# Expert results stored from ScalarE's queue two tiles later, with only weights on SyncE's queue

## What is computed

```python
logits = (xt @ Wr + br) / TEMP
probs = jax.nn.softmax(logits, axis=-1)
w, idx = jax.lax.top_k(probs, TOP_K)
w = w / jnp.clip(jnp.sum(w, axis=-1, keepdims=True), 1e-09)
comb = comb.at[jnp.arange(T)[:, None], idx].add(w)
h = jax.nn.gelu(jnp.einsum('td,edh->teh', xt, W1) + b1, approximate=False)
o = jnp.einsum('teh,eho->teo', h, W2) + b2
y = jnp.einsum('teo,te->to', o, comb)
```

## Time and profile before

| | us |
|---|---|
| median of three runs | 3003.46 (3001.4 to 3005.81) |
| the profiled execution | 2998.74 |
| its span | 2997.0 |
| PE busy | 2473.3 (83%) |
| DVE busy | 1882.4 (63%) |
| ACT busy | 1573.2 (52%) |
| POOL busy | 967.1 (32%) |
| DMA queue of SyncE | 196416 packets, 262.92 MB, 26.1% of 16 engines |

### The profile page before, as it was taken

The page is one execution under the profiler, slowest core; times in us unless marked ns, Lnnn a source line. Parts: engine busy times, 40 slices in busy tenths (PEclk is TensorE's granted clock), DMA queues, the critical chain, the costliest instruction groups (busy, mean ns, idle before and its releaser), DMA issues. The chain is left out here.

```text
span 2997.0 us, 56777 instructions
## 1 busy us (share of the span) xinstructions
PE 2473.3 (83%) x21666; PEld 1595.0 (53%) x21666; DVE 1882.4 (63%) x4197; ACT 1573.2 (52%) x2910; POOL 967.1 (32%) x725
## 2 busy tenths in 40 slices
PE   4489999999999999996877888873799999967724
PEld 2235555555555656554344666651566666744312
DVE  4578777777777766661023766754687887631285
ACT  3336666666666655554132677751377777771121
POOL 2313333333333332223000223335466666550000
PEclk8699999999999999998987899996999999978857
DMA  3301021112111100002102687744433332213020
GB/s 115 95 31 43 29 78 47 36 33 78 47 36 33 62 28 5 5 3 78 71 28 87 232 302 290 286 183 146 159 111 122 111 121 85 86 37 113 20 97 14
DMA packets 197327, 268.64 MB, mean 90 GB/s; under 512 B 48945, under 2 KB 124849, under 8 KB 196545
## 3 DMA queue, kind: packets, MB, share of 16 engines
q1 hardware_dynamic: 196416, 262.92, 26.1%
q0 software_dynamic: 640, 2.10, 0.2%
HBM read 221.18 MB, written 43.78 MB: 88 GB/s over the span
## 5 line engine op out<-in xcount | busy, mean ns | idle before, releaser
L544 POOL TENSOR_TENSOR a_plo<-a_p,a_phi 128x512 bf16<-128x512 f32 x272 | 315.6, 1160 | 815.8 <-ACT a_phi L600 814.5
L734 PE MATMUL ps<-w_hi,a_xhi 128*128 128x512 bf16 x1088 | 415.9, 382 | 0.4 <-DVE a_v L623 0.4
L735 PE MATMUL ps<-w_lo,a_xhi 128*128 128x512 bf16 x1088 | 415.5, 382 | 0.0
L736 PE MATMUL ps<-w_hi,a_xlo 128*128 128x512 bf16 x1088 | 415.2, 382 | 0.0
L1845 POOL TENSOR_TENSOR a_plo<-a_p,a_phi 128x512 bf16<-128x512 f32 x256 | 300.4, 1174 | 199.1 <-ACT a_phi L1882 198.1
L566 ACT ACTIVATE a_kraw<-ps 128x256 f32<-128x256 f32 x272 | 104.2, 383 | 412.6 <-PE ps L736 410.8
L623 DVE TENSOR_TENSOR a_v<-ps,a_v 128x256 bf16<-128x256 f32 x272 | 114.7, 422 | 261.9 <-ACT a_v L568 260.4
L1953 DVE CUSTOM_DVE_ANT_0 a_junk<-ps,a_biasrow 128x512 bf16<-128x512 f32 x256 | 175.8, 687 | 80.4 <-PE ps L2057 77.4
L1877 ACT ACTIVATE a_p<-ps,a_mcol 128x512 f32<-128x512 f32 x256 | 175.0, 684 | 86.4 <-PE ps L2075 80.1
L596 ACT ACTIVATE a_p<-ps,a_mcol 128x512 f32<-128x512 f32 x256 | 175.4, 685 | 57.0 <-PE ps L787 56.9
L1270 POOL TENSOR_TENSOR e_wlo<-e_wst,e_whi 128x2048 bf16<-128x2048 f32 x23 | 112.6, 4895 | 257.3 <-ACT e_whi L1293 257.3
(11 more groups left out here) (436 smaller groups left out, 7214.6 us busy)
## 6 DMA issues: line engine op xcount, KB each, us to landing
e_wst<-in_L_ffn_W SPq DMA_DIRECT2D x46, 2048.0 KB, 11.5
a_xn<-in_ctx SPq DMA_DIRECT2D x16, 1024.0 KB, 5.7
a_ct<-in_ctxT SPq DMA_DIRECT2D x16, 1024.0 KB, 5.5
a_ks<-k1h_d SPq DMA_DIRECT2D x128, 128.0 KB, 2.4
k1h_d<-a_khi SPq DMA_DIRECT2D x64, 128.0 KB, 2.0
k1l_d<-a_klo SPq DMA_DIRECT2D x64, 128.0 KB, 1.7
a_ks<-k1l_d SPq DMA_DIRECT2D x64, 128.0 KB, 2.6
xh_d<-a_xshi SPq DMA_DIRECT2D x48, 128.0 KB, 1.8
```

The costliest lines, as they stand in the source:

```text
L544: pool.tensor_tensor(p_lo[:, m % 3, :], p32[:, m % 2, :], p_hi[:, m % 3, :], ALU.subtract)\
L734: pe.matmul(out, x_hi[:, c, tile], w_hi[:, c, g, :], start=(c == 0), stop=False)
L735: pe.matmul(out, x_hi[:, c, tile], w_lo[:, c, g, :], start=False, stop=False)
L736: last = pe.matmul(out, x_lo[:, c, tile], w_hi[:, c, g, :], start=False, stop=(c == C - 1))
```

## The change

`store` moves from SyncE's queue to ScalarE's. SyncE's loop is left with up_weights and down_weights. In ScalarE's iteration q, behind `gelu_high(q, 1)` and ahead of `gathered(q + 1)`, stands `store(q - 2)`: a wait for `o_done` and the same DMA, with the same semaphore. The last two stores follow the loop. In the kernel before, SyncE's iteration q had `store(q - 1)`.

```diff
--- before.py
+++ after.py
@@ -1227,10 +1227,6 @@
                 src = w2_d[q] if q < E else w2_d[bass.ds(over[q - E], 1)].rearrange("e p c n -> p (e c) n")
                 sp.dma_start(w2(wst, q), src).then_inc(w2_in[q % 2], 16)
 
-            def store(q):
-                sp.wait_ge(o_done, q + 1)
-                sp.dma_start(t["oy_d"][q * P:(q + 1) * P, :], O[:, q % 2, :]).then_inc(o_out[q % 2], 16)
-
             up_weights(0)
             sp.dma_start(wr[:], t["L0_ffn_Wr"].rearrange("(c p) e -> p c e", p=P)).then_inc(small_in, 16)
             sp.dma_start(br[:], row(t["L0_ffn_br"], E)).then_inc(small_in, 16)
@@ -1253,11 +1249,8 @@
                                      .rearrange("p e m -> p (e m)")).then_inc(b1o_in, 16)
                 if q + 2 < TILES:
                     up_weights(q + 2)
-                if q >= 1:
-                    store(q - 1)
                 if q + 2 < TILES:
                     down_weights(q + 2)
-            store(TILES - 1)
 
         @block.gpsimd
         def _(pool):
@@ -1311,6 +1304,10 @@
                 if q >= 2:
                     act.wait_ge(down_mm, q - 1)
                 act.activation(g_hi[:, q % 2, 4 * i:4 * i + 4, :], g32[:, 4 * i:4 * i + 4, :], ACT.Copy).then_inc(ghi, 1)
+
+            def store(q):
+                act.wait_ge(o_done, q + 1)
+                act.dma_start(t["oy_d"][q * P:(q + 1) * P, :], O[:, q % 2, :]).then_inc(o_out[q % 2], 16)
 
             norm.scalar(act)
             turn.scalar(act, ps, HT)
@@ -1335,10 +1332,14 @@
                     up_high(q + 1, 1)
                 gelus(q, range(4, 8))
                 gelu_high(q, 1)
+                if q >= 2:
+                    store(q - 2)
                 if q + 1 < TILES:
                     gathered(q + 1)
                 for i in range(2):
                     down_high(q, i)
+            for q in range(TILES - 2, TILES):
+                store(q)
 
         @block.vector
         def _(dve):
```

## The result

The change makes the kernel slower by 0.23%: medians of 14 runs each are 3012.74 us after and 3005.87 before, the ratio 1.0023 with a 95% interval of 1.0014 to 1.0033. That is 6.9 us (4.2 to 9.9 by the interval), just past the bound of 6.0 that the prediction set between no change and slower. One of the 14 executions before took 4568.69 us, in a slow state, and the ratio leaves it out. The profiled execution after took 3017.1 us with a span of 3015.3. It is 18.4 us over the profiled one of before, and not all of that is the change: the experts' stage (first weight DMA to the first DMA of the next stage) went from 409.1 to 422.9 us, the rest differs by 4.6 us in stages with the same code. I therefore read durations inside the stage from the profiles and the size of the effect from the medians.

What follows compares the result with a forecast made beforehand. A loop of waits, not an engine: pair flight, ScalarE's iteration and GpSimd's half, 29.65 us per two tiles. 10 x 0.64 - 1.1 + 0 = +5.3 us on the 3003.46 median gave 3008.8, range 3000 to 3018.

Steps and rivals of the forecast that it cites:

- case A: Experts' stage: stores moved into the weights' flight cost them bandwidth, +5.3 us, 3008.8; chance 0.50.
- SyncE's queue gives nothing back: SyncE: without the 248.4 us of store waits, pairs still wait for GpSimd's half and leave at the same moment.
- The one exception, 1.1 us saved: SyncE, pair of 1908.27: the store follows a late down_low; without it the pair leaves about 1907.2, 1.1 us saved once.
- the last loop: Experts' stage: of two alternating two-tile loops, the one the end hangs on; ten pairs back from 1970.58 us.
- The transfers, 0.64 us a landing: Weight flights: each store delays the first-layer landing ScalarE awaits by 0.64 us at 411 GB/s; 10 x 0.64 = 6.4 us.
- the 0.87 us: Weight flights: upper price of a store, by the slower rate of the second-layer weights, 300 GB/s.
- ScalarE's queue, 0: ScalarE, behind gelu_high: the long-met o_done wait and the store's issue add 0; 0.5 us a round kept for the range.
- Rival C: ScalarE: the store's issue costs loop time, 0.5 to 1.45 us a round, 5 to 14.5 us on top; chance 0.23.
- The buffer and the end, 0: DVE's result buffer has 15.4 us cover against 2.0 to 5.8 us flight, cost 0; last store 0 to 0.2, taken 0.
- Ten rounds, not twenty: Experts' stage: a gain or loss in a pair's flight or ScalarE's iteration is paid ten times, not twenty.
- The side of the bound: Whole kernel: border at 3009.5, 6.0 us or 0.2%; chances slower 0.47, within 0.46, faster 0.07.

Runs made afterwards that it cites:

- experiment 1: The changed kernel without the stores of tiles 0 to 20, its output tensor filled once in the stage before; ratio 0.9996 to the kernel before.
- experiments 1 to 3: The changed kernel without stores of tiles 0 to 20, with ScalarE's stores cut to an eighth, with each store twice; ratios 0.9996, 0.9994, 1.0056 to the kernel before.
- experiment 4: The kernel before with SyncE's store between a pair's two weight transfers, behind the second-layer weights instead of ahead; ratio 1.0023 to the kernel before.
- experiment 3: The changed kernel with each store issued twice, the second into another DRAM tensor; ratio 1.0056 to the kernel before, 3025.40 against 3007.44 us.

## Why the prediction was right, and where it was not

The measured 3012.7 lies in the range of 3000 to 3018, and case A is what happened. Point by point:

*SyncE's queue gives nothing back.* Right. The wait only changed its name (248.4 us in front of the stores, then 284.2 for GpSimd), and the kernel without any stores is no faster (experiment 1).

*The one exception, 1.1 us saved.* Wrong. I took the pair of 1908.27 as held back by the store. The store was last by 1.1 us there, but the tile was late because GpSimd and DVE had met, and where they meet differs from profile to profile. In the profile after it happened in two tiles of the last loop, with no store in SyncE's way; the first of them on DVE:

```profile
1907.77 4.56 DVE L1368 TENSOR_TENSOR e_gm<-e_ramp,e_ds 128x512 bf16<-128x512 f32 x1
```

The selection matrix (0.69 us elsewhere) took 4.56 beside GpSimd, which had started at 1907.70; down_low ran from 1913.31 to 1915.59 and the pair left at 1915.72, 3.94 us after GpSimd's end, where the kernel before had 3.30. A saving in a place that the next execution doesn't repeat should have had no term in the sum.

*The transfers, 0.64 us a landing.* The mechanism is right: experiments 1 to 3 give landings of 13.63, 13.71, 14.61 and 15.50 us for none, an eighth, one and two stores, and experiment 4 shows it on one ring. The size was off. I took the rate of the first-layer weights (411 GB/s), since it was the rate of the very stretch. A store costs 0.94 us, which is 279 GB/s, and a load of the same shape 1.10. Of the recorded prices the 0.87 us came nearest, but for no reason that holds. It was worked out from the second-layer weights, whose rows in HBM are 2 KB like the store's (the first-layer weights' are 4 KB), and once the stream runs those rows come in at 397 GB/s (the stretch from 1759.51 in experiment 4), which would make 0.66 us. The 411 was read wrongly too: from 1763.5 to 1768.6 the engines moved 287 GB/s and not 2.10 MB, since part of the first-layer weights had come before the second-layer ones landed. That they did move 417 GB/s from 1761.5 to 1766.5 made the number right by luck. What a store costs beyond its own 0.69 us of engine time no rate of the kernel before shows.

With 10 x 0.94 and without the exception the sum would have been +9.4. The measured +6.9, with an interval of 4.2 to 9.9, lies between that and the +5.3 of the forecast and doesn't tell them apart; the landings do. The mean over 19 landings hides one thing more. The ten pairs of the last loop, which a store joins 7 to 9 us after their issue, land 0.73 us later than before, 7.3 us together; the nine others, which it joins after 1 to 4 us, 1.16. Ten rounds at their own price make +7.3.

*ScalarE's queue, 0.* Right, and now shown: 0.33 us of issue under gelu_high, the next activation at 0.53 us. Rival C falls for this change, and experiment 3 shows it where the issue is doubled.

*The buffer and the end, 0.* DVE waits for no store in the profile after, and the stores land within 7.4 us against a cover of 15.4. The 2 to 4 us that I had named for them were too little: 6.3 in the median.

*Ten rounds, not twenty.* Borne out by the profile: the last loop has nine intervals and gained 7.4 us in flights, though both loops' landings rose. It is also why 0.94 us in 19 tiles shows as 6.9 and not as 18.

*The side of the bound.* I gave 0.46 to within 0.2% and 0.47 to slower, with the value at +5.3. The case was the right one, and both errors made the forecast too low: up to 3.0 us too little for the transfers, and 1.1 us credited to the exception. The interval of 4.2 to 9.9 us lies on both sides of the 6.0, so which side is right is not settled.

What stays open: why a store of 0.69 us of engine time delays a landing by 0.73 to 1.16 us. The rate of 2 KB rows by itself doesn't explain it, two queues aren't needed for it (experiment 4), and no run has stores with longer rows. And the tail of the medians: single runs of the changed kernel spread from 3004.6 to 3020.5, those of the kernel before from 3001.4 to 3012.2; the meetings of GpSimd and DVE are a likely cause, but I didn't measure it over many executions.

## What to carry to other kernels

When a queue waits long in front of an operation, look at what it waits for right behind it: if that ends later, taking the first wait away only renames it. A transfer is free or dear by where it lies in time. Ahead of a landing that an engine waits for, it costs its own transfer and more in every round; behind it or in a start-up, on the weights' own queue, it cost nothing that the total shows. And where an engine waits for the same landing in every round, ask first why that transfer wasn't issued earlier. Here turning two issues round gave 31 us, and 44 with one more swap, where moving the stores lost 7.

## What the runs showed of the hardware

- A DMA issue on ScalarE's queue runs while an activation runs: 0.33 us under a 0.63 us activation cost nothing, 0.82 us of issues under the same one cost 0.39.
- A 0.262 MB transfer inside a running 4.2 MB pair delayed it by 0.94 us as a store, 0.89 as a second store and 1.10 as a load; that is 238 to 295 GB/s, where the weights in rows of 2 KB came in at 397 and the store's own packets took 0.69 us of the engines' time.
- Transfers of two queues are not served in the order of their issue: on ScalarE's queue a store issued 1 to 4 us behind a pair landed 4.6 to 7.3 us ahead of that pair's first-layer weights, while on SyncE's own ring behind the pair it took 13.6 us to land. The rule of the Trainium skill that the prediction drew on (*DMA: Bandwidth & Descriptors*, "Issuing engines are not separate DMA queues") has the transfers of all issuing engines run on the same 16 DMA engines and interleave; these landings agree.
- VectorE and GpSimd hold each other up when both work in SBUF: the same down_low took 2.28 or 6.17 us, the selection matrix 0.69 or 4.56, GpSimd's half 4.1 to 5.9, by who started first. In the earlier trace rows GpSimd started at 1900.74 and ended at 1904.97, and DVE, which started at 1900.95, ended 2.15 us after it: it did its work once GpSimd was through. *SBUF — State Buffer* of the Trainium skill, "SBUF: two separate sides", has the two share a pair of ports that the first to start keeps for its whole instruction; these rows agree.
